# A six-stage transformer program: plain turned blocks and the causal projection's copy on ScalarE, the bias as a product of one row, and the first causal heads beside the last feed-forward

## The chip, the cores and the metric

The kernel runs on one core of one Trainium2 chip. The metric is the device time of one execution, in microseconds (us). A core has TensorE (PE in the profile; PEld is its weight load), VectorE (DVE), ScalarE (ACT), GpSimd (POOL) and SyncE (SP, whose queue issues the DMAs). PE writes its results to PSUM, which DVE and ACT read and POOL does not.

## What is computed

Eight sequences of 512 tokens with 256 features, float32, run through four residual layers. Cut to what matters:

```
x = x + latent_attention(layernorm(x))            # stage a, 8 heads
x = x + ffn_block(layernorm(x))                   # two layers f: local attention, feed-forward
x = x + causal_attention(layernorm(x))            # stage b, 16 heads of 16
x = x + ffn_block(layernorm(x))                   # two layers f

causal_attention(x):
    q, k, v = split(x @ w_qkv + b_qkv)
    dot = q @ k.T
    scores = dot * dot / (|q|^2 + |k|^2 - 2 dot + 1e-6)
    out = softmax(scores where key <= query) @ v
    return out @ w_out + b_out
```

## The kernel before

**Stages and units.** `PLAN` lists six stages: a, f, f, b, f, f. A stage runs over the 8 sequences; a stage of one sequence is a unit `u`, so that the causal stage b is units 24 to 31, and unit 23 is the last feed-forward unit before it. Attention is cut into steps: in stage b there are 24 steps `k` a unit. A step takes two heads; three steps (k%3 = 0, 1, 2) cover the query tiles 1 and 0, then 2, then 3 of these heads, with 384, 384 and 512 key columns a head.

**A causal step.** PE computes `bden` (denominators, 18 rows deep) and `bdot` (16 rows deep) into a pair of PSUM banks each (three pairs, `wide0` to `wide2`). DVE bounds the denominators (`bclip`), ACT squares the dots into a `prob` buffer (`bnum`) and makes a first guess of the reciprocal by Ln and Exp (`bguess`). DVE improves the guess (`bclose`, and the first half of `bmul`) and multiplies with a running maximum (second half of `bmul`). ACT takes the exponential (`exp`), PE turns the 128x128 blocks (`turn_a`, `turn_b`, transposes into one PSUM pair), ACT copies the first half to the buffer `pt` (`pt_a`, line 1209), DVE the second (`pt_b`): blocks on the diagonal times a 0/1 mask (line 1408), and for k%3 = 2 two blocks below the diagonal as a plain copy (line 1411). PE then forms the output (`mix`). `bclip`, `bguess`, `bclose` and `bmul` share three buffers `b_den` and `b_inv`, which lie in rooms (`w_up`, `x_2`, `hid`) that the feed-forward uses too.

**The projection of stage b.** For each of 4 token tiles PE forms 128x768 of q, k and v (`bqkv`: two halves of the depth, 512 and 256 columns each). DVE adds the bias, which a DMA has spread over all 128 rows of `w_in`, and writes the tile to `raw` (`row`, line 1324). ACT squares q and k (`bsq`, line 1144) and copies v to its place (line 1147), DVE sums the squares (`bss`, line 1331), and POOL puts q, k and the sums in rows (`brow`). After the four tiles PE turns the rows (`bk`, `bq`), ACT copies them (`bk_c`, `bq_c`), and SP copies the halves crosswise by DMA (`dup_a`, `dup_b`).

**The ends of a unit.** `sel`, `olog`, `osum`, four `fan` (PE, a product of 16 rows into the one bank `turn_ps`) and `out_b` (DVE, line 1425) normalise the output of a unit; `proj` and `res` (DVE, line 1431) add it to x. In a feed-forward unit follow `moved` (DMA), `bn_f`, `bn_f2`, `nrm_f`, `xt2`, three `up_g` with `gate`, `gelu` (ACT), three `up_h` with `hid`, four `down`, `res2` (DVE, line 1494), and `back` (POOL, line 1593).

**The order.** Nothing is issued by hand. `parts_of` lists the parts of each unit with a due time and what each follows; `cost` gives a length to each; `ordered` builds for each engine one fixed order. It always takes, among the parts that can start within `PATIENCE` (0.3) of the earliest, the one with the lowest due time, and gives PSUM rooms to PE's parts as their readers free them. The engines run these orders in program order, each waiting on semaphores. In stage b `bclip`, `bguess`, `bden` and the DMAs of the first steps follow unit 23's last `up_h`, `down` and `back`, since their buffers lie in that unit's rooms:

```
put("bden", k, at, ..., last, *turned, ("down", u - 1, 3))
put("bclip", k, at, final("bdot", k), ("bmul", *three), ("up_h", u - 1, 2))
put("bguess", k, at + .5 / steps, final("bclip", k), ("bmul", *three), ("down", u - 1, 3), ("back", u - 1, 0))
```

## Time and profile before

| | us |
|---|---|
| median of 3 runs (4489.77 to 4497.48) | 4490.21 |
| the profiled execution's own time | 4488.74 |
| its span, from first to last instruction | 4486.5 |
| stage b, from the first causal product to the next stage alone (about 1991 to 3150 in the span) | 1158.6 |

The time of an execution is its span and 2.24 us around it here. The page's first part gives each engine's busy time, the second cuts the span in 40 slices with the clock granted to TensorE, and the fifth lists groups of instructions by line. A line of a helper (823 for every product, 826 for every transpose, 1603 for every DMA) stands for many operations, so these are told apart by the names of their tiles and by their shapes. A product in float32 stands as two MATMUL records, a transpose as one.

### The profile page before, as it was taken

How to read it: one execution, taken by the hardware profiler on the slowest of the kernel's cores; microseconds unless marked ns; L12 is line 12 of the kernel's file. 1: busy time of each engine (PE TensorE's matmuls, PEld its weight loads, DVE VectorE, ACT ScalarE, POOL GpSimd, SP SyncE). 2: the span in 40 equal slices, each digit the busy share in tenths (PEclk: the TensorE clock that was granted, in tenths of full speed). 3: DMA queues.
4: the chain of work that ended last, by engine and by line, in shares of the span. 5: the costliest groups of instructions: out<-in, count | busy, mean ns of one | idle time of the engine just before them, and what ended most of it. 6: DMA issues, size and time to landing. Idle time of an engine off the chain costs nothing.

```text
span 4486.5 us, 65884 instructions
## 1 busy us (share of the span) xinstructions
PE 4149.7 (92%) x23120; PEld 2608.4 (58%) x23120; DVE 3315.1 (74%) x7977; ACT 2541.7 (57%) x5478; POOL 1658.1 (37%) x1816
## 2 busy tenths in 40 slices
PE   8999989999999999988888887888999999999997
PEld 5666556566566566555555555554566665665664
DVE  5667777777667667559999999998677776677662
ACT  4555554454454454439888888876454454454441
POOL 1222365445446456330000010013464464465541
PEclk9999999999999999987888889888999999999998
DMA  2000000000010000000000000101000000100000
GB/s 75 10 16 6 24 10 6 3 3 6 23 29 12 11 8 11 23 21 20 20 22 20 20 23 22 34 20 34 3 6 3 3 25 8 34 15 17 15 17 21
DMA packets 63095, 78.33 MB, mean 17 GB/s; under 512 B 15344, under 2 KB 47520, under 8 KB 62768
## 3 DMA queue, kind: packets, MB, share of 16 engines
q1 hardware_dynamic: 62768, 74.12, 5.8%
q8 instruction: 186, 3.05, 0.3%
q14 instruction: 141, 1.16, 0.1%
HBM read 36.37 MB, written 12.58 MB: 11 GB/s over the span
## 4 chain that ended last, share of the span: by engine, by line
PE 63%; DVE 23%; issue 6%; ACT 4%; POOL 2%; DMA 0%; SPq 0%; POOLq 0%; DVEq 0%; ACTq 0%
PE wide L823 43%; PE o_ps L823 7%; PE wide L826 6%; PE turn_ps L826 4%; DVE x L1246 3%; DVE turned L1297 2%; DVE w_up L1359 2%; PE turn_ps L823 2%; DVE prob L1371 2%; DVE x L1365 2%; DVE prob L1382 2%; DVE w_up L1344 1%; POOL prob L1575 1%; DVE turned L1283 1%; DVE hid L1365 1%
## 5 line engine op out<-in xcount | busy, mean ns | idle before, releaser
L823 PE MATMUL wide<-x,w_up 128*128 128x512 f32 (+5 forms) x2560 | 856.6, 552 | 5.5 <-DVE x L1463 4.1
L823 PE MATMUL wide<-w_in,x_t 128*128 128x512 f32 (+2 forms) x1920 | 811.7, 566 | 15.8 <-ACT q_t L1122 8.3
L1575 POOL TENSOR_SCALAR prob<-prob,st 128x256 f32<-128x256 f32 (+1 forms) x1024 | 496.3, 503 | 821.7 <-DVE st L1395 819.1
L1182 ACT ACTIVATE prob<-prob,st 128x256 f32<-128x256 f32 (+1 forms) x1024 | 479.2, 471 | 251.5 <-DVE st L1382 251.2
L823 PEld LDWEIGHTS wide<-w_in,x_t 128*128 128x128 f32 x1920 | 341.4, 192 | 368.6 <-issue 359.0
L823 PEld LDWEIGHTS wide<-x,w_up 128*128 128x128 f32 (+2 forms) x2560 | 377.2, 198 | 291.9 <-issue 279.3
L823 PE MATMUL o_ps<-pt,v 128*32 128x128 f32 (+2 forms) x5120 | 509.3, 345 | 16.8 <-DVE pt L1411 5.4
L1548 POOL TENSOR_TENSOR sines<-raw,rot 128x512 f32<-128x512 f32 x256 | 351.4, 1393 | 336.7 <-ACT raw L1110 336.4
L1556 POOL TENSOR_TENSOR rn<-ss,minus_half 128x16 f32<-128x16 f32 x128 | 423.1, 3305 | 103.3 <-DVE ss L1292 96.3
L823 PEld LDWEIGHTS o_ps<-pt,v 128*64 128x64 f32 (+1 forms) x5120 | 326.8, 133 | 227.1 <-issue 143.4
L1213 ACT ACTIVATE o_t<-o_ps 128x512 f32<-128x512 f32 x192 | 114.4, 596 | 521.2 <-PE o_ps L823 521.0
L1382 DVE CUSTOM_DVE_ANT_0 prob<-wide,local_mask 128x256 f32<-128x256 f32 (+1 forms) x1024 | 331.6, 384 | 61.3 <-PE wide L823 58.5
L823 PE MATMUL wide<-k_t,q_t 64*128 64x256 f32 (+2 forms) x2456 | 367.7, 413 | 1.7 <-DVE pt L1415 0.8
L823 PE MATMUL wide<-w_out,o_t 128*128 128x256 f32 x1536 | 351.7, 388 | 4.0 <-ACT o_t L1213 1.9
L826 PE MATMUL turn_ps<-ident,prob 128*128 128x128 f32 x1916 | 311.2, 280 | 31.1 <-ACT pt L1209 15.9
L826 PE MATMUL wide<-ident,prob 128*128 128x128 f32 x1844 | 294.1, 305 | 48.8 <-issue 15.6
L823 PE MATMUL wide<-hid 18*128 18x256 f32 (+3 forms) x1024 | 227.0, 531 | 120.5 <-DVE pt L1408 28.5
L823 PE MATMUL wide<-w_down,hid 128*128 128x256 f32 (+1 forms) x1536 | 332.7, 388 | 4.8 <-DVE hid L1486 4.8
L823 PEld LDWEIGHTS wide<-w_out,o_t 128*128 128x128 f32 x1536 | 298.8, 196 | 62.1 <-issue 14.8
L826 PEld LDWEIGHTS turn_ps<-ident,prob 128*128 128x128 f32 x1916 | 223.8, 141 | 183.7 <-issue 152.8
L1486 DVE SCALAR_TENSOR_TENSOR hid<-wide,bias_up,hid 128x512 f32<-128x512 f32 (+1 forms) x224 | 144.8, 669 | 250.7 <-ACT hid L1232 138.7
L826 PEld LDWEIGHTS wide<-ident,prob 128*128 128x128 f32 x1844 | 228.6, 155 | 164.5 <-issue 120.3
(153 smaller groups left out, 7490.1 us busy)
## 6 DMA issues: line engine op xcount, KB each, us to landing
kept<-resid SPq DMA_DIRECT2D x16, 512.0 KB, 3.0
x<-kept SPq DMA_DIRECT2D x16, 512.0 KB, 3.3
w_up<-hid SPq DMA_DIRECT2D x64, 128.0 KB, 2.2
x<-hid SPq DMA_DIRECT2D x64, 128.0 KB, 2.4
shifted<-resid SPq DMA_DIRECT2D x32, 224.0 KB
w_in<-in_f_wqkv SPq DMA_DIRECT2D x4, 1536.0 KB, 6.3
w_up<-in_f_w SPq DMA_DIRECT2D x4, 1492.0 KB, 6.7
resid<-in_x SPq DMA_DIRECT2D x8, 512.0 KB, 8.9
```

Of the source, the lines that this page charges most:

```text
L823: return eng.matmul(out, lhsT, rhs, start=start, stop=stop, skip_group_check=True)
L826: return eng.transpose(out, in_, ident[:, :])
L1182: last = eng.activation(pr[:, local_span(t)], pr[:, local_span(t)], ACT.Exp, bias=sm[:, t:t + 1], scale=-1.0, accum_out=sm[:, 4 + t:5 + t])
L1213: eng.activation(o_t[:, i, :], o_ps[:, :], ACT.Copy).then_inc(S["out"], 1)
L1246: return eng.tensor_scalar(dst, src, stat[:, 64 + 2 * t:65 + 2 * t], stat[:, 96 + t:97 + t], ALU.subtract, ALU.mult)
L1297: eng.tensor_tensor(out[:, :], out[:, :], sines[(o - 1) % 2][:, :], ALU.add).then_inc(S["add"], 1)
L1365: eng.scalar_tensor_tensor(out=inv, in0=den, scalar=2.0, in1=inv, op0=ALU.subtract, op1=ALU.mult).then_inc(S["binv"], 1)
L1382: eng.tensor_tensor_reduce(pr[:, local_span(t)], ps[:, local_span(t)], local_mask[:, P if t == 0 else 0:256], -1.0, LOW, ALU.add, ALU.min, ...
L1486: last = eng.scalar_tensor_tensor(out=hid[rows, m, cols], in0=ps[rows, 512 * k + cols.start:512 * k + cols.stop], scalar=bias_up[rows, m:m ...
L1548: last = eng.tensor_tensor(halves(sines[(o - 1) % 2][:, side]), halves(r[:, side])[:, :, ::-1, :], rot[:, 2 * z + 1, i, :].rearrange("p (u ...
L1556: eng.tensor_tensor(rn[(o - 1) % 2][:, 0:16], ss[(o - 1) % 2][:, 0, :], minus_half[:, 0:16], ALU.pow).then_inc(S["rn"], 1)
L1575: last = eng.tensor_scalar(pr[:, local_span(t)], pr[:, local_span(t)], sm[:, 8 + t:9 + t], 1.0, ALU.mult, ALU.mult)
```

## The change

Four edits, and the planner's tables with them.

1. **Plain blocks by ScalarE.** For k%3 = 2 the two blocks below the diagonal are copied by ACT in a new part `pt_c`, which waits for `pt_b` (DVE, the masked blocks of the same bank) and for which `mix` and the reuse of the PSUM pair wait.
2. **The bias by a product.** The bias stays one row; a row of ones (`one_row`, a new input) is loaded beside it, and PE adds the bias by a product of depth 1 with 512 and 256 columns at the end of each `bqkv`.
3. **The copy by ScalarE.** `row` moves from DVE to ACT, and copies q and k alone (512 columns). `bsq` reads PSUM in place of `raw`, and no longer waits for `row`; the PSUM pair is held until both are done.
4. **The first causal heads.** The steps k = 0, 1, 2 of unit 24 take other buffers (`prob2`, `prob3`, `sines`), and no longer wait for unit 23's `down`, `up_h` and `back`. They run one at a time there (each waits for the `bmul` of the step before). The parts of unit 23's feed-forward get the due time 23.9 each.

The core of the diff:

```diff
+def early(u, k):
+    return u == FIRST_B and k < 3
+def early_group(u, k):
+    return u == FIRST_B and k < 6
...
+        if early(u, k):
+            n_prob = 2
...
-        "ACT": "fold_q_c xt_c raw v_c q_c aq_c av_c bsq bk_c bq_c bnum bguess exp pt_a out olog gelu",
-        "DVE": "fold_o_c bn_h nrm_h cos ss join k_c ak_c row bss bclip ...
+        "ACT": "fold_q_c xt_c raw v_c q_c aq_c av_c bsq row bk_c bq_c bnum bguess exp pt_a pt_c out olog gelu",
+        "DVE": "fold_o_c bn_h nrm_h cos ss join k_c ak_c bss bclip ...
...
-            put("bsq", i, at, final("row", i), ("bss", *back1), ...
+            put("bsq", i, at, final("bqkv", i), ("bss", *back1), ...
...
-            put("bden", k, at, final("bk_c", g), final("bq_c", g), final(dup, g), last, *turned, ("down", u - 1, 3))
+            ffn = [] if early(u, k) else [("down", u - 1, 3), ("up_h", u - 1, 2), ("back", u - 1, 0)]
+            put("bden", k, at, final("bk_c", g), final("bq_c", g), final(dup, g), last, *turned, *ffn[:1])
...
-            put("bclip", k, at, final("bdot", k), ("bmul", *three), ("up_h", u - 1, 2))
+            if early(u, k):
+                three = (u, k - 1)
+                ffn = [("turn_a", u - 1, STEPS["f"] - 1), ("turn_b", u - 1, STEPS["f"] - 1)]
+            put("bclip", k, at, final("bdot", k), ("bmul", *three), *ffn)
...
+            if k % 3 == 2:
+                put("pt_c", k, at + 2 / steps, final("pt_b", k), *mixed)
-            put("mix", k, at + 3 / steps, final("pt_a", k), final("pt_b", k), final("bsq", 3), o_free)
+            put("mix", k, at + 3 / steps, final("pt_a", k), final("pt_b", k), final("pt_c", k), final("bsq", 3), o_free)
...
+    after = lambda late: u + .9 if u == FIRST_B - 1 else u + 1 + late
...
-                            last = mm(ps[:, lo:lo + w], x_t[:, c, 1 + i * P:1 + (i + 1) * P], w_in[:, at:at + w],
-                                      c == 0, c == FC - 1)
+                            mm(ps[:, lo:lo + w], x_t[:, c, 1 + i * P:1 + (i + 1) * P], w_in[:, at:at + w], c == 0, False)
+                    for lo, w in ((0, 512), (512, 256)):
+                        last = mm(ps[:, lo:lo + w], one_row, qkv_bias[:, lo:lo + w], False, True)
...
+                elif kind == "row":
+                    act.wait_ge(S["bqkv"], o)
+                    act.wait_ge(S["brow"], o - 2)
...
+                    eng.activation(raw[(o - 1) % 2][:, 0:2 * DIM], wide[PLACE["bqkv", u, i]][:, 0:2 * DIM], ACT.Copy
+                                   ).then_inc(S["row"], 1)
                 elif kind == "bsq":
-                    act.wait_ge(S["row"], o)
+                    act.wait_ge(S["bqkv"], o)
...
+                elif kind == "pt_c":
+                    act.wait_ge(S["pt_b"], nth("pt_b", u, i))
+                    met, n = P * B_OWN[i % 3], P * len(B_TURNS[i % 3][1])
+                    eng.activation(prob_t[SLOTS[u, i]["pt"]][:, 512 + met:512 + n],
+                                   wide[PLACE["turn_b", u, i]][:, 512 + met:512 + n], ACT.Copy).then_inc(S["pt_c"], 1)
...
-                elif kind == "row":
-                    row = raw[(o - 1) % 2]
...
-                    eng.tensor_tensor(row[:, 0:3 * DIM], wide[PLACE["bqkv", u, i]][:, 0:3 * DIM], qkv_bias, ALU.add
-                                      ).then_inc(S["row"], 1)
...
-                        if n > met:
-                            last = eng.tensor_copy(pt[:, 512 + met:512 + n], ps[:, 512 + met:512 + n])
```

The fixed orders differ only from unit 22 to unit 34. Two places show how.

**PE, between the attention of unit 23 and its `down`.** `wide<-x_2,w_up` are the feed-forward's `up_g` and `up_h`, `wide<-w_in,x_t` the causal projection, `w_down,hid` is `down`. Before, behind the last `up_g` tile:

```order
L823 MATMUL wide1<-x_2,w_up 106x256 x4
L823 MATMUL wide1<-x_2,w_up 128x512 x2
L823 MATMUL wide2<-w_in,x_t 128x512
L823 MATMUL wide2<-w_in,x_t 128x256
L823 MATMUL wide2<-w_in,x_t 128x512
L823 MATMUL wide2<-w_in,x_t 128x256
L823 MATMUL wide0<-x_2,w_up 128x512 x4
L823 MATMUL wide2<-x_2,w_up 128x512 x4
L826 MATMUL wide1<-ident,turned0 128x128 x8
L823 MATMUL wide0<-w_down,hid 128x256 x24
```

and with the change (`sines` hold the first causal rows, `w_in` alone is the product of one row):

```order
L876 MATMUL wide0<-w_in,x_t 128x512
L876 MATMUL wide0<-w_in,x_t 128x256
L876 MATMUL wide0<-w_in,x_t 128x512
L876 MATMUL wide0<-w_in,x_t 128x256
L876 MATMUL wide0<-w_in 128x512
L876 MATMUL wide0<-w_in 128x256
L876 MATMUL wide2<-x_2,w_up 128x512 x4
L876 MATMUL wide1<-x_2,w_up 128x512 x4
L876 MATMUL wide0<-sines0 128x512 x2
L876 MATMUL wide2<-sines1 128x512 x2
L876 MATMUL o_ps<-pt0,v0 32x128 x6
L876 MATMUL wide1<-w_down,hid 128x256 x24
```

The products of step 2 and the `mix` of step 0 (and in front of this piece the products of steps 0 and 1 and the transposes of step 0) now stand ahead of `down`; the transposes of unit 26's layernorm (`ident,turned0`) and, further on, two of its four projections, which stood there or right behind, come later.

**ACT, around a `bsq` and a step with k%3 = 2 in the middle of unit 27.** Before:

```order
L1163 ACTIVATE prob0<-wide1 128x768
L1144 ACTIVATE turned1<-raw0 128x512
L1147 ACTIVATE v0<-raw0 128x16x16
L1209 ACTIVATE pt1<-wide0 128x256
L1174 ACTIVATE x_2<-w_up 128x768
L1176 ACTIVATE x_2<-x_2 128x768
L1163 ACTIVATE prob1<-wide1 128x768
```

and with the change:

```order
L1199 ACTIVATE raw0<-wide1 128x512
L1206 ACTIVATE turned1<-wide1 128x512
L1209 ACTIVATE v0<-wide1 128x16x16
L1270 ACTIVATE pt1<-wide0 128x256
L1260 ACTIVATE st3<-st3 128x2
```

and a dozen rows further on

```order
L1270 ACTIVATE pt1<-wide0 128x512
L1235 ACTIVATE hid<-w_up 128x1024
L1237 ACTIVATE hid<-hid 128x1024
L1274 ACTIVATE pt1<-wide0 128x256
L1227 ACTIVATE prob3<-wide2 128x768
```

`row` (L1199) stands in one piece with `bsq`, all three reading the same PSUM pair, and `pt_c` (L1274) stands two activations behind its step's `pt_a`. The ACT order also holds two more table loads (61 before, 63 now): unit 23's `gelu` now stands between causal steps, with a load ahead of it and one behind.

## Rows read from the trace of the kernel before

**Rows 1.** Page: busy shares, and granted clock in 40 slices

```profile
PE 4149.7 (92%) x23120; PEld 2608.4 (58%) x23120; DVE 3315.1 (74%) x7977; ACT 2541.7 (57%) x5478; POOL 1658.1 (37%) x1816
...
PEclk9999999999999999987888889888999999999998
```

**Rows 2.** Windows; us, then PE, PEld, DVE, ACT, POOL busy, clock, DMA, GB/s

```profile
2000.00:2100.00 100.00, 80.07 (x653) 51.80 (x646) 98.98 (x233) 95.97 (x171) 0.00 (x0) 0.76 0.09 21
...
1991.40:3150.00 1158.60, 954.31 (x7022) 602.23 (x7024) 1071.48 (x2448) 969.14 (x1725) 126.98 (x160) 0.85 0.09 23
```

**Rows 3.** Windows of one causal sequence (137.5 us), and of its parts

```profile
2411.00:2548.50 137.50, 112.32 (x857) 71.10 (x856) 128.94 (x296) 117.74 (x208) 11.19 (x18) 0.87 0.08 20
...
2421.00:2509.00 88.00, 66.29 (x588) 43.62 (x588) 86.38 (x208) 83.05 (x148) 5.33 (x13) 0.92 0.10 25
...
2509.00:2538.40 29.40, 25.93 (x172) 14.09 (x170) 27.45 (x59) 25.25 (x44) 5.87 (x5) 0.85 0.08 19
...
2538.40:2558.00 19.60, 19.60 (x100) 13.04 (x98) 15.21 (x33) 9.44 (x17) 0.00 (x0) 0.70 0.00 1
```

**Rows 4.** Waits over two sequences, 2411 to 2687 us: total, times, longest

```profile
DVE o_t L1425 <- PE turn_ps L823: 7.1, 5, 2.6
...
ACT st L1199 <- DVE st L1371: 16.5, 19, 2.2
```

**Rows 5.** Groups of the stretch 2421 to 2509 us: count, busy, mean ns, idle before

```profile
L1365 DVE SCALAR_TENSOR_TENSOR x<-w_up,x 128x768 f32<-128x768 f32 x12 | 11.4, 951 | 0.2
...
L1365 DVE SCALAR_TENSOR_TENSOR hid<-w_up,hid 128x1024 f32<-128x1024 f32 x5 | 6.1, 1211 | 0.0
...
L1324 DVE TENSOR_TENSOR raw<-wide,w_in 128x768 f32<-128x768 f32 x3 | 2.9, 950 | 0.0
...
L1411 DVE COPY pt<-wide 128x256 f32<-128x256 f32 x6 | 2.5, 412 | 0.0
```

**Rows 6.** Groups by form, 1950 to 2850 us

```profile
L1209 ACT ACTIVATE pt<-wide 128x256 f32<-128x256 f32 x51 | 19.2, 377 | 10.1 <-PE wide L826 9.9
...
L1209 ACT ACTIVATE pt<-wide 128x512 f32<-128x512 f32 x100 | 58.7, 587 | 2.4 <-PE wide L826 2.3
...
L823 PE MATMUL wide<-hid 18*128 18x256 f32 x208 | 48.7, 489 | 50.3 <-DVE pt L1411 17.1 <-ACT prob L1163 11.3 <-issue 9.6
```

**Rows 7.** Timelines of DVE and ACT: start, us, what, idle before it

```profile
2506.81 0.41 DVE L1411 COPY pt<-wide 128x256 f32<-128x256 f32 x1
...
2507.14 1.22 DVE L1359 TENSOR_TENSOR w_up<-w_up,hid 128x1024 f32<-128x1024 f32 x1
...
2518.62 0.96 DVE L1324 TENSOR_TENSOR raw<-wide,w_in 128x768 f32<-128x768 f32 x1 [1.61 <-PE wide L823]
...
2003.51 0.38 ACT L1209 ACTIVATE pt<-wide 128x256 f32<-128x256 f32 x1
...
2003.78 0.20 ACT L1199 ACTIVATE st<-st 128x2 f32<-128x2 f32 x1
```

**Rows 8.** Timeline of PE: a projection's tile, and one fan product

```profile
1987.48 2.75 PE L823 MATMUL wide<-w_in,x_t 128*128 128x512 f32 x8
...
2545.08 1.91 PE L823 MATMUL turn_ps<-shifted,w_down 16*128 16x512 f32 x2
```

**Rows 9.** The change of stage: window, and PE, DVE, POOL, SP timelines

```profile
1922.90:1991.40 68.50, 63.38 (x229) 39.51 (x230) 38.00 (x87) 14.55 (x27) 28.98 (x43) 0.98 0.11 25
...
1973.71 10.34 PE L823 MATMUL wide<-w_down,hid 128*128 128x256 f32 x48 [0.72 <-DVE hid L1486]
...
2003.07 0.42 DVE L1344 TENSOR_SCALAR w_up<-wide 128x256 f32<-128x256 f32 x1
...
2007.67 0.69 DVE L1371 CUSTOM_DVE_ANT_0 prob<-prob,hid 128x512 f32<-128x512 f32 x1
...
1985.46 2.35 POOL L1593 TENSOR_TENSOR resid<-resid,x 128x1024 f32<-128x1024 f32 x1 [7.05 <-DVE resid L1494]
...
1988.34 0.56 SPq L1603 DMA_DIRECT2D w_up<-hid  x1
```

More of the change, by code:

```diff
@@ L152, in cost @@
         n = len(B_TURNS[i % 3][kind[-1] == "b"])
-        return {"turn": 0.03 + 0.152 * n, "pt_a": 0.06 + 0.117 * n, "pt_b": (0.2 if i % 3 == 2 else 0.1) + 0.118 * n}[
+        return {"turn": 0.03 + 0.152 * n, "pt_a": 0.06 + 0.117 * n, "pt_b": 0.1 + 0.118 * (2 if i % 3 == 2 else n)}[
             "turn" if kind[0] == "t" else kind]
+    if kind == "pt_c":
+        return 0.3
     if kind in B_COST and st == "b":
@@ L304, in parts_of @@
                     free = (u, 6 * (g - 1) - 1) if g >= 2 else (u - 1, 6 * (g + 3) - 1)
-                    put(kind + "_c", g, at - 4 / steps, final(kind, g), ("bdot", *free), ("down", u - 1, 3))
+                    put(kind + "_c", g, at - 4 / steps, final(kind, g), ("bdot", *free),
+                        ("join" if early_group(u, k) else "down", u - 1, 3))
                 for half in range(2):
@@ L374, in parts_of @@
         return out
-    put("bn_f", 0, u + 1, final("res"), ("nrm_f", max(v for v in range(-1, u) if v < 0 or stage_of(v) == "f"), 0))
-    put("moved", 0, u + 1, final("res"), ("nrm_f", u - 1, 0))
-    put("bn_f2", 0, u + 1, final("bn_f"), final("moved"), ("pad_down", n * SEQS, 0))
-    put("rstd_f", 0, u + 1, final("bn_f2"))
-    put("nrm_f", 0, u + 1, final("rstd_f"), ("bmul", u - 1, BSTEPS - 1), ("xt2", u - 1, 0), ("back", u - 1, 0))
-    put("bias", 0, u + 1.2, final("nrm_f"), ("load_up", n * SEQS, 0))
@@ L382, in parts_of @@
-    put("xt2", 0, u + 1.2, final("nrm_f"))
-    put("xt2_c", 0, u + 1.2, final("xt2"), ("up_h", u - 1, 2), ("load_up", n * SEQS, 0))
+    after = lambda late: u + .9 if u == FIRST_B - 1 else u + 1 + late
+    put("bn_f", 0, after(0), final("res"), ("nrm_f", max(v for v in range(-1, u) if v < 0 or stage_of(v) == "f"), 0))
+    put("moved", 0, after(0), final("res"), ("nrm_f", u - 1, 0))
+    put("bn_f2", 0, after(0), final("bn_f"), final("moved"), ("pad_down", n * SEQS, 0))
+    put("rstd_f", 0, after(0), final("bn_f2"))
@@ L439, in readers_of @@
     if kind == "turn_a" and stage_of(u) == "b":
-        last.append(("pt_b", u, i))
+        last += [("pt_b", u, i), ("pt_c", u, i)]
     if kind == "score" and stage_of(u) == "f":
@@ L573 @@
         "load_fold fold_q fold_q_c fold_o fold_o_c aq aq_c lat ak_c av_c bqkv row bsq bv bss brow bk bk_c bq bq_c bias_b "
-        "score bden bdot low inv exp wt wt_b bclip bnum bln bguess bclose binv bmul turn_a turn_b neg pt_a pt_b mix sel fan out olog oexp osum out_b load_sel "
+        "score bden bdot low inv exp wt wt_b bclip bnum bln bguess bclose binv bmul turn_a turn_b neg pt_a pt_b pt_c mix sel fan out olog oexp osum out_b load_sel "
         "proj res moved bn_f bn_f2 var_f rstd_f nrm_f bias xt2 xt2_c up_g gate gelu up_h hid down res2 back_in back store "
@@ L637, in build, with rows_home, close_home, close_free @@
         k_rows = [b_hid[:, 1024 + 512 * i:1536 + 512 * i] for i in range(2)]
+        early_rows = [sines[0][:, 0:512], sines[0][:, 512:1024], sines[1][:, 0:512], sines[1][:, 512:1024]]
+        def rows_home(u, g):
+            return early_rows if early_group(u, 6 * g) else [q_rows[g % 2], k_rows[g % 2], q_half, k_half]
+        def close_home(u, i):
+            pair = [prob["prob2"], prob["prob3"]] if early(u, i) else [a[(nth("bguess", u, i) - 1) % 3] for a in (b_den, b_inv)]
+            return [a[:, 0:2 * b_width(i)] for a in pair]
+        def close_free(gate, u, i):
+            if early(u, i):
+                gate.wait_ge(S["bmul"], nth("bmul", u, i) - 1)
+                gate.wait_ge(S["turn_a"], nth("turn_a", u - 1, STEPS["f"] - 1))
+                gate.wait_ge(S["turn_b"], nth("turn_b", u - 1, STEPS["f"] - 1))
+            else:
+                gate.wait_ge(S["bmul"], nth("bmul", u, i) - 3)
+                if u == FIRST_B:
+                    gate.wait_ge(S["down"], nth("down", u - 1, TILES - 1))
+                    gate.wait_ge(S["up_h"], nth("up_h", u - 1, len(UP_H) - 1))
+                    gate.wait_ge(S["back"], nth("back", u - 1))
         b_weight = shifted[0:BHEADS, :, :].rearrange("p t n -> p (t n)")
@@ L1162, in scalar_program @@
                     prob_free(act, u, i)
+                    if u == FIRST_B and not early(u, i):
+                        act.wait_ge(S["bmul"], nth("bmul", u, 2))
                     eng.activation(two(prob[SLOTS[u, i]["prob"]][:, 0:2 * w], slice(0, w)),
```

110 lines of the change are left out of this document (56 added, 54 removed).

## The prediction

> **What bounds the kernel now.** I read the page first. PE is busy for 92% of the span, DVE for 74%, ACT for 57% [rows 1], so PE seems to be the bound. It is not everywhere. The slices of granted clock fall below 9 from the 18th on for about a quarter of the span [rows 1], and the windows show why: in the causal stage b DVE is busy for 99 us of a window of 100 us, ACT for 96, PE for 80 [rows 2]. Over the whole stage of 1158.6 us DVE is busy 1071.5 (92%), ACT 969.1 (84%), PE 954.3 (82%) [rows 2]. The change works in this stage and at its start, so its worth is read there.
>
> One causal sequence takes 137.5 us, with 128.9 of DVE, 117.7 of ACT and 112.3 of PE [rows 3]. It has two kinds of stretch. In a long one of 88 us nothing but steps runs: DVE 86.4 (98%), ACT 83.1 (94%), PE 66.3. Around the sequence's end the next 29.4 us have DVE at 27.5, ACT at 25.3 and PE at 25.9, and in the last 19.6 us PE never rests while DVE is busy for 15.2 and ACT for 9.4, at a mean granted clock of 0.70 [rows 3]. DVE's waits are in this last part: 7.1 us in two sequences for the fan products [rows 4]. ACT's waits are for DVE: 16.5 us in two sequences for the maxima of `bmul` [rows 4]. So DVE is the bound of the long stretch, with ACT close behind it, and PE of the last one.
>
> **Term 1, DVE.** The plain copy goes: 412 ns each [rows 5], but the next instruction starts 0.33 us after it [rows 7], and that is what it occupies. 8 a sequence, 64 in all: 21.1 us. `row` goes: 950 ns each [rows 5], 0.87 us with the same overlap of 0.08, 4 a sequence, 32 in all: 27.8 us. DVE also waited 1.61 us for PE ahead of one of them [rows 7], a wait that goes to ACT. Together 6.1 us of 128.9 a sequence.
>
> **Term 2, ACT.** `pt_c` is the copy of 256 columns that ACT makes already for k%3 = 0: 377 ns [rows 6], 0.27 us to the next start [rows 7]; 64 of them, 17.3 us. `row` now copies 512 columns: 587 ns for that form [rows 6], less the same overlap of 0.11 us, 0.48 us; 32 of them, 15.4 us. `bsq` and the copy of v read PSUM in place of SBUF; I count no gain or loss for them. That is 4.1 us more a sequence: 121.8, against 122.8 for DVE. The two engines become equal.
>
> What the row shows here is that for this copy out of PSUM ACT is not slower than DVE (377 against 412 ns). The Trainium skill (ScalarE: Activation LUTs, Rules for kernel authors) says that additions and the like should go to VectorE, which per element is up to about three times faster in bf16; by that the 64 copies would cost ACT some 79 us in place of 17, and ACT would be far above DVE. The trace disagrees for float32 from PSUM, and the sum keeps its rows.
>
> **Term 3, PE.** A projection tile streams 2 x 768 columns in 2.75 us at full clock [rows 8]. The products of one row stream 768 more: 1.37 us, 32 times, 44 us on PE. No row has a product of depth 1. The nearest, the fan product of 16 rows, takes 1.91 us for 512 columns where the clock stands at the lower level [rows 8], so few rows save nothing, and 768 columns would take 2.8 us there. Bounds: 1.37 and 2.8 us; I take 1.37, since most tiles lie where the clock is mostly full. In the long stretch PE is idle for 21.7 of 88 us [rows 3], which hides it. If that cover were gone, it would be 4 times 1.4 to 2.8 us a sequence.
>
> **Term 4, the held pair.** `pt_c` waits for `pt_b`, and `mix` and the PSUM pair for both. Before, the pair was free 0.33 us after the masked product; now after a hop to ACT, whatever ACT is doing, and 0.38 us. PE's products of the next step waited on the old copy for 17.1 us in 900 [rows 6]. So this wait exists already, 0.3 us a time. I count nothing, because PE has 25% to spare in these stretches; its bounds are 0 and one ACT instruction (1 us) a time, 8 us a sequence.
>
> **Term 5, the change of stage.** From the end of unit 23's attention to the first causal product PE is busy 63.4 of 68.5 us, DVE only 38.0, ACT 14.6 [rows 9]. `down` ends at 1984.05 [rows 9]. Now eight products of one row (11.0 us) and about half the PE work of three steps (a step has about 4 us of PE in the long stretch, 66.3 us for its 17 steps [rows 3, 5]; so 6 us) stand ahead of that end, and unit 26's transposes (1 us) behind it: it comes 16 us later, at about 2000. `res2` and `back` (1.4 us to the start of `back`, and 2.35, [rows 9]) then hold step 3 until about 2004, against 2003.07 before; but steps 0 to 2 are through DVE by then, which before was at 2008.4 [rows 9]. What is gained by DVE is the work between (about 4 us), less 1. The two extra table loads are on ACT, which is idle there. On SP four DMAs of the first heads are now ahead of `moved`, 0.56 us each to issue [rows 9], up to 2.3 us; PE has unit 25's projections to do meanwhile. I take 0 for the whole, with bounds of 5 us either way: the early heads pay for the products of one row, no more.
>
> **The sum.** Long stretch (17 steps, 12 and 5 of them by the widths of line 1365, with 6 plain copies and 3 `row`, [rows 5]): DVE falls by 6 x 0.33 + 3 x 0.87 = 4.6 to 81.8, ACT rises by 6 x 0.27 + 3 x 0.48 = 3.1 to 86.1. ACT is now the higher. Filled to 98% as DVE is today, it needs 87.9 us, a gain of 0.1; if it were no bound, DVE at 98% would need 83.5, a gain of 4.5. I take 99%, which DVE reaches in a window where ACT has 96% [rows 2]: 87.0 us, a gain of 1.0. End of the sequence: DVE loses one `row` with its wait (0.87 + 1.61) and two copies (0.66), 3.1 us; PE is nearly full there, so 1.4 of that goes to the product of one row. A gain of 1.7. Together 2.7 us a sequence, 8 sequences: 22 us. Against the profiled execution's 4488.7 that is 4466.7; the median of the runs stands 1.5 us above it, so **4468**.
>
> **The rivals.**
> - **A, the forecast: ACT and DVE share the bound.** 15 to 30 us faster, 4460 to 4475. For it: the balance of the two sums. Chance 0.40.
> - **B, DVE's relief comes through whole.** ACT's waits for DVE (8 us a sequence, [rows 4]) show it has room that opens as DVE gets faster, and 4 to 6 us a sequence come out: 32 to 48 us, 4442 to 4458. Against it: ACT at 94 to 96% already. Chance 0.27.
> - **C, ACT takes DVE's place.** ACT in order, at 122 us with 12 us of unavoidable waits, gives 134 to 137.5 with the later PSUM pairs eating the rest: within 9 us, 4481 to 4494. The early heads may also do nothing, since they only trade places with unit 26's projections. Chance 0.18.
> - **D, PE becomes the bound: slower.** The place is the sequence's end, where PE never rests. At the lower clock a product of one row costs 2.8 us; and in the trace the clock falls to that level after the fan products, which are 16 rows deep. If the products of depth 1 bring more time at the lower level, as after the fans, PE does its work there at twice the time. It decides when PE's work plus this passes DVE's relief of 6.1 us a sequence: four tiles with 1.4 more each make 5.6, and half of the 5.9 us of clock that the last stretch loses now (0.30 of 19.6 us, [rows 3]) makes it 8.5. The loss is 2.4 to 3 us a sequence, some 22 in all, 4512. Against it: PE's 25 us of idle a sequence. Chance 0.15. The Trainium skill (TensorE: Matmul & The Clock Gate, Part 4) says that a transpose does not count as busy for the clock in the way a product does. Stage b, full of transposes, has a mean clock of 0.85 [rows 2], which agrees, and no row tells whether a depth of 1 counts.
>
> That the change does not do what it says I leave out: the orders show each part moved.
>
> **How the numbers follow.** 0.2% of the time, 9 us, is about what a measurement of this kernel tells from no change. Faster by more: nearly all of A and B, 0.66, and a little of C, 0.68. Within: most of C and the edge of A, 0.18. Slower: D less what it may turn to nothing, 0.14. The range of 8 in 10 runs from the middle of B, 4442, to the upper edge of C, 4493; the forecast's own is 4458 to 4476.
>
> **What would show it.** In the page after: DVE's busy time lower by about 55, ACT's higher by about 43 us, PE's by 44 or more. In the windows of a sequence in mid-stage: about 134.8 us, DVE 122 to 123, ACT 122. In the groups: a one-row product of 512 columns as long as other products of 512; `pt_c` near 380 ns. In the waits: DVE's wait ahead of `row` gone, and PE's `<-DVE pt L1411` now on ACT, no longer in total. At the change of stage: `down` ending near 2000, step 3 at about 2004. The prediction is wrong if sequences stay at 137 us with ACT above 95% throughout (C), if they fall below 132 (B), or if the mean clock of stage b falls under 0.82 (D).

## The result, and the profile after

The changed kernel takes **4543.31 us** (median of 4 runs, 4539.49 to 4547.61) against 4489.99 for the kernel before on the same chip: ratio **1.0117**, 95% interval 1.0104 to 1.013, a loss of 53 us. The forecast was 4468, the range 4442 to 4493: wrong in sign, and outside the range. Even the slower rival, D, stood at 4512.

The page of the kernel after (span 4543.0 us; the profiled execution took 4544.86), with its busy shares, its granted clock in 40 slices and the shares of the chain that ended last:

```profile
PE 4224.6 (93%) x23248; PEld 2639.0 (58%) x23248; DVE 3278.2 (72%) x7881; ACT 2576.7 (57%) x5576; POOL 1659.2 (37%) x1816
...
PEclk9999999999999999997888888888999999999999
...
PE 66%; DVE 16%; ACT 9%; issue 6%; POOL 2%; DMA 0%; SPq 0%; POOLq 0%; DVEq 0%; ACTq 0%
```

Against [rows 1] DVE has 37 us less, ACT 35 more and PE 75 more, where 55, 43 and 44 were foretold. To place the loss I cut the stage by the 1.22 us addition of `res` that ends each sequence's attention. Its starts in units 24 and 30 are 2149.18 and 2970.38 us before, 2161.61 and 3033.16 after. So the stage stands 12 us later at the end of its first sequence and **loses 50 us in the six sequences that follow** (821 against 872). Of the 12, 5.5 were there before anything differed: the fixed orders differ only from unit 22 on, and the `back` of unit 21 started at

```profile
1839.47 2.36 POOL L1593 TENSOR_TENSOR resid<-resid,x 128x1024 f32<-128x1024 f32 x1 [0.65 <-DVE resid L1494]
```

before and, after, at

```profile
1844.96 2.36 POOL L1645 TENSOR_TENSOR resid<-resid,x 128x1024 f32<-128x1024 f32 x1 [0.64 <-DVE resid L1546]
```

At this point the twenty profiled executions of all kernels here lie between 1838.2 and 1845.0, so starts in two traces are compared by their distance from it. At unit 31's `res` the changed kernel is 65 us behind (3126.06 and 3191.39); the rest of the span gives 9 of them back, which leaves the 56.5 of the two profiled spans. The windows of the six sequences (us, then PE, PEld, DVE, ACT, POOL busy, clock, DMA, GB/s), before:

```profile
2149.00:2970.00 821.00, 676.11 (x5157) 430.56 (x5158) 774.28 (x1772) 706.75 (x1248) 67.42 (x106) 0.87 0.09 23
```

and after, with one sequence in the middle (from `res` of unit 27 to that of unit 28) behind it:

```profile
2161.00:3033.00 872.00, 738.67 (x5285) 457.89 (x5283) 751.15 (x1709) 731.66 (x1325) 63.26 (x108) 0.85 0.08 22
...
2595.00:2744.00 149.00, 125.05 (x895) 77.61 (x894) 128.17 (x289) 123.95 (x224) 14.01 (x22) 0.84 0.09 23
```

The sequence of 137.5 us with DVE at 94% [rows 3] has become this one of 149 us with DVE at 86%, ACT at 83% and PE at 84%: nobody is full, and it is slower. It is one of the longer ones; from `res` to `res` the six take 145.3 us on average, 136.9 before. DVE did get its relief (774 to 751). PE is busy for 62.6 us more, while its idle time went from 145 to 133 us. So the loss of 51 is PE's busy time less 12 of idle; that is a sum and not yet a cause. The one-row products of these 24 tiles make 41 of the 63 (26.9 and 14.2 in the rows below), and the rest goes with a clock of 0.85 in place of 0.87. The groups of the kernel after by form, 1950 to 2850 us, show the new operations (count, busy, mean ns, idle before them):

```profile
L876 PE MATMUL wide<-w_in 1*128 1x512 f32 x48 | 26.9, 640 | 0.0
L1274 ACT ACTIVATE pt<-wide 128x256 f32<-128x256 f32 x47 | 17.3, 367 | 2.8 <-DVE pt L1462 2.8
...
L876 PE MATMUL wide<-w_in 1*128 1x256 f32 x48 | 14.2, 374 | 0.0
L1199 ACT ACTIVATE raw<-wide 128x512 f32<-128x512 f32 x24 | 14.1, 589 | 25.0 <-PE wide L876 25.0
```

Their sizes are as foretold: `pt_c` 367 ns (377 [rows 6]), the row copy 589. The largest of PE's waits from 1990 to 3100 us (total, times, longest), after:

```profile
PE o_ps L876 <- ACT pt L1274: 33.4, 20, 2.7
PE wide L879 <- ACT pt L1274: 27.1, 15, 2.9
PE wide L876 <- ACT pt L1274: 19.6, 9, 3.0
PE wide L876 <- DVE w_up L1400: 14.1, 16, 1.8
```

and before, in the same stretch:

```profile
PE wide L823 <- DVE pt L1408: 28.7, 20, 2.6
PE wide L823 <- DVE w_up L1346: 18.8, 23, 1.8
PE wide L823 <- DVE pt L1411: 18.4, 6, 3.5
```

80 us of PE's waits now end with `pt_c` (L1274), and 12 more with DVE's mask (L1462); before, 61 ended with DVE's two turned copies (47 in the rows above, the rest in four smaller ones). The timeline shows how one arises (start, us, engine, what, idle before it):

```profile
2339.36 0.59 ACT L1270 ACTIVATE pt<-wide 128x512 f32<-128x512 f32 x1
...
2339.84 1.06 ACT L1235 ACTIVATE hid<-w_up 128x1024 f32<-128x1024 f32 x1
2340.02 0.42 DVE L1462 TENSOR_TENSOR pt<-wide,causal_keep 128x256 f32<-128x256 f32 x1
...
2340.93 1.06 ACT L1237 ACTIVATE hid<-hid 128x1024 f32<-128x1024 f32 x1
...
2341.89 0.37 ACT L1274 ACTIVATE pt<-wide 128x256 f32<-128x256 f32 x1
...
2342.40 1.97 PE L876 MATMUL wide<-w_in,x_t 128*128 128x512 f32 x2 [1.36 <-ACT pt L1274]
```

DVE's mask is done at 2340.44, but ACT has the Ln and Exp of the next `bguess` (2 x 1.06 us) ahead of `pt_c` in its fixed order, and the PSUM pair comes free 1.8 us after the mask. In the plan 61 of the 64 `pt_c` stand directly behind a `bguess`. My first theory was this handover, with the one-row products and the early heads as rivals.

### The profile page after: what moved, and what is told of

Read it like the earlier page. It is cut to its first block, busy times and chain, and to the rows that moved or that the text cites. A ratio compares the mean times of both kernels' runs of the same rounds, so it can differ in the third digit from the quotient of the medians.

```text
span 4543.0 us, 66166 instructions
## 1 busy us (share of the span) xinstructions
PE 4224.6 (93%) x23248; PEld 2639.0 (58%) x23248; DVE 3278.2 (72%) x7881; ACT 2576.7 (57%) x5576; POOL 1659.2 (37%) x1816
## 4 chain that ended last, share of the span: by engine, by line
PE 66%; DVE 16%; ACT 9%; issue 6%; POOL 2%; DMA 0%; SPq 0%; POOLq 0%; DVEq 0%; ACTq 0%
PE wide L876 45%; PE o_ps L876 8%; PE wide L879 7%; PE turn_ps L879 4%; DVE x L1312 2%; DVE turned L1363 2%; PE turn_ps L876 2%; ACT prob L1263 2%; DVE prob L1436 1%; POOL prob L1627 1%; ACT prob L1227 1%; ACT pt L1270 1%; DVE turned L1366 1%; ACT hid L1235 1%; DVE turned L1349 1%
## 5 line engine op out<-in xcount | busy, mean ns | idle before, releaser
L876 PE MATMUL wide<-w_in,x_t 128*128 128x512 f32 (+2 forms) x1920 | 834.5, 580 | 30.9 <-ACT pt L1274 14.2
L876 PE MATMUL wide<-x,w_up 128*128 128x512 f32 (+3 forms) x2528 | 856.3, 551 | 3.1 <-DVE x L1515 1.7
L876 PEld LDWEIGHTS wide<-w_in,x_t 128*128 128x128 f32 x1920 | 351.0, 197 | 396.5 <-issue 386.1
L876 PEld LDWEIGHTS wide<-w_down,hid 128*128 128x128 f32 (+1 forms) x1536 | 255.1, 189 | 55.6 <-issue 22.1
```

What stands on the lines that cost most here:

```text
L876: return eng.matmul(out, lhsT, rhs, start=start, stop=stop, skip_group_check=True)
```

## The experiments

Eighteen kernels ran. Differences in us are the ratio less 1, times 4490; the interval in brackets behind each ratio is a 95% interval, and one of plus or minus 0.0015 is 7 us. A difference between two of these kernels carries both intervals, about 9 us. The table at the end of this section has all of them.

### The edits apart (e1 to e4)

The edits of the diff were taken as three (the one-row products and ScalarE's row copy together are the bias edit), singly and in combination; the planner orders each anew. `e1_without_plain` is the changed kernel with the `pt_c` edit undone:

```
-                put("pt_c", k, at + 2 / steps, final("pt_b", k), *mixed)
...
+                        if n > met:
+                            last = eng.tensor_copy(pt[:, 512 + met:512 + n], ps[:, 512 + met:512 + n])
```

> The changed kernel with the plain blocks given back to VectorE (no pt_c; mask and plain copy both at pt_b); the one-row products, ScalarE's row copy and the early heads stay. Theory P (the handover VectorE to ScalarE holds the mix and the PSUM pair: in the changed kernel PE idles some 60 us of 1950 to 2850 behind L1274): most of the loss of 53 us goes, 4470 to 4500 us. Rival Q (the one-row products, 640 ns a record of 512 columns where I had counted less, make PE the bound and bring the clock down): the loss stays, 4530 to 4550. Rival R (the early heads disturb the order of the whole stage): also 4530 or more here, and the run with the early heads alone is slower as well.

`e2_plain_alone`, the kernel before with only the `pt_c` edit:

> The kernel before with one edit alone: the plain blocks of every third head by ScalarE as pt_c. Theory P: slower than before by 30 to 50 us (4520 to 4540), with PE idle behind the pt_c line and the sequences of the causal stage at 143 to 150 us. Rivals Q and R: VectorE loses 64 x 0.33 = 21 us and nothing is added to PE, so 4465 to 4490.

`e3_bias_alone`, only the one-row products and ScalarE's copy:

> The kernel before with one edit alone: the bias by products of one row, the copy of 512 columns by ScalarE. Theory P: VectorE is relieved by 28 us, PE gets 45 us that mostly lie in its idle time: 4470 to 4495. Rival Q: slower, 4510 to 4540, PE busy in the causal stage over 90% and its clock lower for longer.

`e4_early_alone`, only the early heads:

> The kernel before with one edit alone: the first three causal heads may run beside the last feed-forward. Theory P: 4480 to 4495, the step between the two stages moves by under 10 us. Rival R: 4505 or more, mostly at the change of stage, where the changed kernel's end of the last feed-forward came 20 us later.

Measured: e1 1.0019 (1.0006 to 1.0031), e2 1.0004 (0.9988 to 1.002), e3 1.0056 (1.0034 to 1.0077), e4 1.0005 (0.9991 to 1.002). The handover as sole cause falls: alone it costs nothing measurable. The bias edit alone costs 25 us. The plan of e2 has 62 of its 64 `pt_c` directly behind a `bguess`, as the changed kernel's has 61, so that place alone isn't what costs. Early heads alone do nothing, and e1, which has them, is only 9 us slower than before: R falls. But the parts don't add up: the plain copy costs nothing beside the old code or beside the early heads (`v4_plain_and_early`, 1.0005, 0.9995 to 1.0015), and 44 us beside the bias edit and the early heads (1.0117 against 1.0019). Of the combinations one did not run: plain copy and bias edit without the early heads.

> The kernel before with the plain blocks by ScalarE and the early heads, and without the bias edit. Each of the two alone moved the time by under 3 us. If the order made with the plain copy in it goes bad only beside the one-row products: 4485 to 4500. If it goes bad with the early heads: 4515 or more.

The early heads have a use after all: from the `back` of unit 21 to `res` of unit 24 e3 takes 319.5 us and e1 305.6, where the kernel before takes 309.7. So they give back 14 us at the change of stage, where the bias edit had cost 10. Both are small for one trace: orders of the old computation (o1 to o3 below) spread from 304.5 to 316.6 us at this place. In the whole time the early heads are worth 16 us there (1.0056 against 1.0019).

### One operation out, the order untouched (e5, e6, f3)

To tell operations from order, the next kernels keep the changed kernel's order, place for place. `e5_no_products` leaves out the products:

```
-                    for lo, w in ((0, 512), (512, 256)):
-                        last = mm(ps[:, lo:lo + w], one_row, qkv_bias[:, lo:lo + w], False, True)
...
```

> The changed kernel, its order untouched, without the one-row products: the bias of the causal projection is left out of the computation (its load stays), 64 records of PE less. The four runs before this one showed that the plain blocks alone and the early heads alone move nothing and that the bias edit alone costs 24 us, so the theories are put anew. Theory Q (PE's time: 2 x 0.5 us a tile, 32 tiles, and the clock that falls with them): 4500 to 4520 here, 25 to 45 us less than the changed kernel. Rival O (the cost lies in the order that the planner makes from the new set of parts, and in its waits between engines): 4535 to 4545, under 10 us less.

`e6_plain_back` keeps the products, lets DVE do the plain copy behind its mask, and leaves ACT's place empty:

```
                 elif kind == "pt_c":
...
+                    pass
...
+                        if n > met:
+                            last = eng.tensor_copy(pt[:, 512 + met:512 + n], ps[:, 512 + met:512 + n])
```

> The changed kernel, its order untouched, with the plain copy done by VectorE right behind the mask, and ScalarE's place for it left empty. Theory H (the handover from VectorE to a ScalarE whose queue holds the 2.1 us of the next Ln and Exp ahead of it costs some 1 us a head on PE's path, 64 heads): 4495 to 4515. Rival O (the order itself): 4535 to 4555, since VectorE gets its 21 us back and the order stays.

Measured: e5 1.0042 (1.0025 to 1.0058), 34 us below the changed kernel. e6 1.0092 (1.0076 to 1.0108), 11 us below it. So giving the handover back is worth 11 us here (by the two intervals, 2 to 20), and that is net of the 64 copies that DVE does again; leaving the products out is worth 34. But e6 holds the same instructions as e1 (PE x23248, DVE x7945, ACT x5512 in both pages), and e1 is 33 us faster: **the order and the PSUM places that the planner makes when `pt_c` is among its parts cost three times what the handover itself does.** The traces put 16 of them in the six sequences (842 and 858 us) and 12 between unit 21's `back` and unit 24's `res` (305.6 and 317.4 us). `f3_neither` takes both the handover and the products out of the changed kernel's order:

> The changed kernel's order with both parts of its cost taken out: the plain copy by VectorE, ScalarE's place for it empty, and no one-row products (the bias is left out of the computation). If the two parts add up (34 and 11 us apart): 4495 to 4502, and what is left above before is the order and ScalarE's place in the bias edit. If they cover each other: 4503 to 4510.

It took 1.0095 (1.0076 to 1.0113): not faster than e6, and 24 us slower than e5. Neither of the two foretold sums came. In this order the products cost 34 us where ScalarE copies the blocks and nothing where DVE does, and giving the copy back to DVE gains 11 with the products and loses 24 without them. No run leaves the copy out altogether in this order. Six sequences of e5, of e6 and of f3:

```profile
2146.00:3000.00 854.00, 697.28 (x5196) 440.29 (x5198) 752.02 (x1711) 729.44 (x1326) 67.06 (x108) 0.85 0.09 22
```

```profile
2162.00:3020.00 858.00, 730.36 (x5272) 454.55 (x5270) 765.92 (x1759) 719.16 (x1282) 69.10 (x108) 0.85 0.08 22
```

```profile
2152.00:3021.00 869.00, 713.50 (x5173) 449.37 (x5170) 765.63 (x1758) 720.44 (x1278) 71.47 (x108) 0.83 0.08 22
```

From e6 to f3 PE loses its products but only 17 us of busy time, because the clock falls from 0.85 to 0.83, and it idles 27 us more (155 against 128). The clock's fall isn't a chance of one execution: over the whole span the four executions of e6 have 0.949 to 0.953, the four of f3 0.945 or 0.946.

### One operation in or out, in the order of before (b1, v1, e8)

`b1_products_only` puts the one-row products into the kernel before, loads the bias as one row, and turns DVE's addition into a copy at the same place:

```
-                    eng.tensor_tensor(row[:, 0:3 * DIM], wide[PLACE["bqkv", u, i]][:, 0:3 * DIM], qkv_bias, ALU.add
-                                      ).then_inc(S["row"], 1)
+                    eng.tensor_copy(row[:, 0:3 * DIM], wide[PLACE["bqkv", u, i]][:, 0:3 * DIM]).then_inc(S["row"], 1)
...
```

> The kernel before, its order untouched, with the bias as one-row products and VectorE's addition over 768 columns turned into a copy over the same columns at the same place: PE's part of the edit alone. Theory Q (PE's time and clock): 4505 to 4520. Rival O: 4488 to 4500, the 32 x 1.0 us of PE lying in its idle time.

Measured 1.0047 (1.0027 to 1.0067), 21 us (12 to 30). The page says PE is busy for 4195.9 us, 46.2 more than before: 1.44 us a tile, of which 0.66 us shows in the time. The groups of b1, 1950 to 2850 us, have the products beside the deep ones of the same 24 tiles:

```profile
L823 PE MATMUL wide<-w_in,x_t 128*128 128x512 f32 x96 | 54.2, 648 | 0.0
L823 PE MATMUL wide<-w_in,x_t 128*128 128x256 f32 x96 | 29.0, 384 | 0.0
L823 PE MATMUL wide<-w_in 1*128 1x512 f32 x48 | 26.9, 640 | 0.0
L823 PE MATMUL wide<-w_in 1*128 1x256 f32 x48 | 14.2, 374 | 0.0
```

By these rows the products themselves are 41.1 us for 24 tiles, 1.71 us each.

`v1_no_plain_copy` takes DVE's plain copy away and puts nothing in its place: the relief of DVE with no price. It leaves those blocks uncopied.

```
-                        if n > met:
-                            last = eng.tensor_copy(pt[:, 512 + met:512 + n], ps[:, 512 + met:512 + n])
```

> The kernel before, its order untouched, with VectorE's copy of the plain blocks left out of the computation (64 copies of 412 ns; the mask multiplication stays, and nothing takes the copy's place). If VectorE's time bounds the causal stage: 4465 to 4470, 20 to 25 us less than before. Rival L (the stage is bound by a ring of waits among the engines in their fixed order, in which PE's time counts as well): 4478 to 4492, under half of it.

Measured 0.9984 (0.9975 to 0.9994): **7 us (3 to 11) for 64 copies of 412 ns**, 21 by my count. This is the run that decides over the forecast. Four sequences of before:

```profile
2282.00:2830.00 548.00, 448.72 (x3436) 285.43 (x3436) 516.26 (x1185) 470.66 (x832) 46.91 (x75) 0.87 0.08 21
```

and of v1:

```profile
2288.00:2831.00 543.00, 460.57 (x3425) 291.72 (x3424) 506.15 (x1152) 471.58 (x832) 46.58 (x75) 0.84 0.08 22
```

DVE lost 10.1 us, the stretch 4 (547.2 to 543.2 from `res` to `res`), and PE, with the same work, is 11.9 us busier at a clock of 0.84 in place of 0.87. This last is one execution against one, and too little to build on: over the whole span the ten executions of v1 have a clock of 0.953 to 0.956 and the 21 of before beside them 0.952 to 0.959, means of 0.954 and 0.955. Where the other 14 us of DVE's relief went these two traces don't say.

`e8_plain_old_order` puts `pt_c` right behind `pt_a`, in the order of before:

> The kernel before, its order untouched, with the plain copy by ScalarE right behind its copy of the other half of that head, where it waits for VectorE's mask with ScalarE's queue behind it. If VectorE bounds the stage and the handover costs little when no Ln and Exp stand before it: 4470 to 4482. If the bound is the ring of waits among three engines and not VectorE's time: 4488 to 4500. If the handover costs a microsecond a head wherever it stands: above 4510.

Measured 1.0244 (1.0228 to 1.026), 110 us. The wait is where the handover was put, and ACT's queue stands behind it. ACT's waits from 2150 to 3050 us:

```profile
ACT pt L1220 <- DVE pt L1420: 81.8, 46, 6.9
ACT prob L1170 <- PE wide L829: 54.6, 24, 6.1
```

So the place behind Ln and Exp, which I had blamed, was far better than this one.

### The rest of the bias edit (v3)

`v3_act_copy_no_bias` is e3 without its products, in the same fixed order:

> The bias edit alone (4516 us) without its one-row products: the bias is left out of the computation, ScalarE copies the 512 columns, VectorE has no addition. Theory Q (the loss of the edit is PE's time): 4488 to 4496, as before or a little less. If ScalarE's place in the edit costs by itself: 4505 or more. If VectorE's relief of 28 us counts in full: 4465.

Measured 1.0031 (1.0019 to 1.0042), 14 us slower than before, between the foretold values. Of the 25 us of e3 the products are 11 (about 0 to 22, by the two intervals); and 14 remain with DVE relieved by 28 and PE having no more to do. Its six sequences:

```profile
2154.00:2991.00 837.00, 707.00 (x5157) 445.35 (x5156) 758.63 (x1744) 711.61 (x1273) 71.56 (x108) 0.83 0.09 23
```

PE does the work of before (x5157 in both) in 31 us more, at 0.83 where it was 0.87. Here the other executions agree: over the whole span the six of v3 have a clock of 0.947 to 0.952, the 21 of before beside them 0.952 to 0.959. Idle time fell by 15 us at once (145 to 130), and the window grew by 16. The order is another than before's, so how much of this is ScalarE's place and how much the order stays open.

### Is it the luck of one order? (o1 to o4)

Three kernels keep the computation of before and give the planner the changed kernel's numbers, so that in 326 to 454 places of PE's, ACT's and DVE's orders another part stands. The first (o1) changes one number, the second (o2) gives the projection's parts the changed kernel's (`bqkv` 4.2 for 3.3, `bsq` 0.8 for 0.82, `row` 0.52 for 0.85), the third (o3) both, and a fourth kernel (o4) plans the changed computation with other numbers. The edit of o1:

```
-"pt_b": (0.2 if i % 3 == 2 else 0.1) + 0.118 * n
+"pt_b": 0.1 + 0.118 * (2 if i % 3 == 2 else n)
```

> The kernel before with nothing of its computation changed: only the planner's number for the turned copy is the changed kernel's (pt_b of every third head 0.34 instead of 0.67), so the order of the causal stage is another. If the planned order by itself is worth tens of microseconds: off by more than 10 us from before, on either side. If orders of the same instructions are all about as good, and what costs is the handover and PE's time: within 7 us of before.

> As the last, with the changed kernel's numbers for the bias edit (bqkv 4.2, bsq 0.8, row 0.52) and the computation of before. The bias edit without its products cost 15 us though it relieved VectorE by 28. If those 15 are the order that these numbers make: 4500 to 4515. If they are ScalarE's place in the edit: 4483 to 4495.

> Both sets of numbers at once, the computation of before. Order theory: another value again, more than 10 us from before or from the two runs ahead. Otherwise within 7 us of before.

> The changed kernel's computation in full, planned with other numbers (bqkv 3.3 instead of 4.2, pt_c 0.4 instead of 0.3). If the 31 us between the two orders of one computation (plain copy at VectorE: 4532 in the changed kernel's order, 4500 in its own) are the luck of one order: 4505 to 4530. If they belong to any order that hands the plain copy over beside the one-row products: 4535 to 4550.

Measured: o1 0.9992 (0.9979 to 1.0006), o2 0.9997 (0.9986 to 1.0008), o3 1.0006 (0.9995 to 1.0016); o4 1.0095 (1.008 to 1.0111). Orders of the old computation differ by a few us in the whole time; their six sequences spread more (821, 817 and 833 us, against 821 before). The changed computation, ordered with other numbers, gains 10 on the changed kernel and still loses 43. So it is hardly the luck of one order: all three orders made for parts with both edits (after, o4 and h10 below) lose 43 us or more, and the one order of e1, without `pt_c`, 9.

### The place of the handover (h10, g10)

One number of the plan moves the turned copies forward, `pt_c` with them:

```
-                put("pt_" + side, k, at + 2 / steps, final("turn_" + side, k), *mixed)
+                put("pt_" + side, k, at + 1.0 / steps, final("turn_" + side, k), *mixed)
...
```

> The changed kernel with one number of the plan changed: pt_a, pt_b and pt_c fall due one step's share earlier, so the mask comes earlier at VectorE, and pt_c stands behind the Ln and Exp of bguess in 22 places of 64, not in 61. If that place is what makes the handover and the order dear: 4500 to 4525. If any order with the handover beside the products costs as much: 4530 to 4550.

> The same earlier due times with the plain copy by ScalarE and the early heads, without the bias edit (behind bguess in 19 places of 64 instead of 61; 4491 us with the old due times). If the place of the handover is what ate the relief of VectorE: 4470 to 4485, the best so far. If VectorE's relief is worth nothing anyhow: 4486 to 4500.

Measured: h10 1.0167 (1.015 to 1.0185), 22 us slower than the changed kernel; g10 1.0022 (1.001 to 1.0035), 8 us slower than v4. Getting most of the handovers out from behind Ln and Exp made both worse. Both runs move every turned copy and so the whole order, so they don't price the place by itself; but with e2 and v4, which have 62 and 61 of 64 in that place and lose nothing, and with e6, they leave nothing for that theory.

### All runs

Windows are six sequences, from `res` of unit 24 to that of unit 30; PE idle is the window less PE's busy time. "Order" tells whose plan it is. Each window is of the one profiled execution (that of e2 took 4502.7 us, 11 more than the median of its ten), and orders of one computation spread from 817 to 833 here, so the ratio decides and not the window.

| run | what it is | order | ratio | us from before | window | PE busy | PE idle | DVE busy | clock |
|---|---|---|---|---|---|---|---|---|---|
| before | | own | 1 | 0 | 821 | 676 | 145 | 774 | 0.87 |
| v1 | no plain copy | before | 0.9984 | -7 | 818 | 686 | 132 | 760 | 0.86 |
| b1 | products | before | 1.0047 | +21 | 829 | 702 | 127 | 777 | 0.88 |
| e8 | `pt_c` at `pt_a` | before | 1.0244 | +110 | 913 | 733 | 180 | 760 | 0.80 |
| e2 | `pt_c` | own | 1.0004 | +2 | 826 | 696 | 130 | 757 | 0.84 |
| e4 | early heads | own | 1.0005 | +2 | 820 | 676 | 144 | 774 | 0.87 |
| v4 | `pt_c`, early | own | 1.0005 | +2 | 824 | 691 | 133 | 756 | 0.85 |
| g10 | v4, earlier due | own | 1.0022 | +10 | 837 | 685 | 152 | 761 | 0.84 |
| v3 | ACT's row copy | own | 1.0031 | +14 | 837 | 707 | 130 | 759 | 0.83 |
| e3 | that and products | own | 1.0056 | +25 | 841 | 725 | 116 | 756 | 0.86 |
| e1 | e3 and early | own | 1.0019 | +9 | 842 | 720 | 122 | 761 | 0.87 |
| e6 | as e1 | after | 1.0092 | +41 | 858 | 730 | 128 | 766 | 0.85 |
| f3 | e6, no products | after | 1.0095 | +43 | 869 | 714 | 155 | 766 | 0.83 |
| e5 | all, no products | after | 1.0042 | +19 | 854 | 697 | 157 | 752 | 0.85 |
| after | all | own | 1.0117 | +53 | 872 | 739 | 133 | 751 | 0.85 |
| o4 | all, other numbers | own | 1.0095 | +43 | 864 | 717 | 147 | 752 | 0.87 |
| h10 | all, earlier due | own | 1.0167 | +75 | 886 | 767 | 119 | 748 | 0.80 |

(o1, o2 and o3: -4, -1, +3.) Read the columns together: every kernel with `pt_c`, with ACT's row copy or with the copy left out has DVE 8 to 26 us less busy, and none but v1 has a shorter window, by 3 us. No version beat both kernels by more than a measurement can tell, unless it left work out.

## Why the prediction was wrong

**"So DVE is the bound of the long stretch" failed first, and with it the step from busy time to time.** The sum let a stretch be as long as the busy time of its fullest engine, filled to 99% as in one window of 100 us [rows 2], and at the sequence's end it took DVE's relief less one product as time. From 49 us of relief at DVE against 33 more on ACT it so got its 22. The changed kernel's six sequences are filled to 86% by DVE and to 84% by ACT (751 and 732 of 872 us): the busy times came about as forecast (ACT 121.9 us a sequence for 122, DVE 125.2 for 122 to 123), the fill did not. v1 measures the step by itself, with no load moved anywhere: 21 us off DVE, 7 gained. v3, with 28 of the relief and no products, was 14 slower. My reading is that the engines, in fixed orders through one another's results, are members of a ring, of which DVE at 98% was the fullest, with ACT at 94% beside it; no run shows the ring as such. And PE's time isn't fixed: in v3 and in f3 it did the same or less work at a lower granted clock.

**Term 1 and term 2: near.** DVE fell by 37 on the page, where the sum had 49 and the sign to look for 55: v1 lowers it by 18 and v3 by 25, near the 21 and 28 of the sum, and the changed kernel has less than these two together. ACT rose by 35 (33 in the sum, 43 as the sign), and `pt_c` took 367 ns. The page of the Trainium skill (ScalarE: Activation LUTs, Rules for kernel authors) would keep additions and the like off ScalarE, with its factor of three for bf16; carried over to these float32 copies, which its rule doesn't name, it gave my estimate of 79 us, and the run shows 64 x 0.37 = 24, with 367 ns on ScalarE where DVE took 412. So the factor doesn't hold for this copy. It would have led to the right sign by a wrong mechanism.

**Term 3: the duration was a quarter short, "hides it" was wrong.** 1.37 us a tile was taken, the price at the full clock; the products' own rows give 1.71, within the bounds of 1.37 and 2.8. PE's idle time was to hide it. It hid all of it from e6 to f3, and let 11 us through in e3 against v3, 21 in b1, and 34 in the changed kernel against e5. That a product stands in front of the operand that a waiting engine needs next is my reading of this; no row isolates it.

**Term 4, "I count nothing", failed.** Its upper bound, one ACT instruction a time, was too low as well: in the timeline above it is two. Yet in the changed order the handover costs 11 us net (e6), 0.17 us a copy, which lies within the bounds of the term as a whole (0 to 64); most of the 80 us of waits took the place of others, for PE's idle time fell. What had no term at all is that the planner, given `pt_c` as a part and the pair held for it, makes another order for the whole stage: 33 us (e6 against e1).

**Term 5: 0 within 5 us.** Right for the early heads by themselves (e4), and right that they pay for the products (e3 to e1, 14 us at that place). In the whole change `down` ends at 2004.55 and step 3 starts at 2009.26; less the 5.5 us by which this execution was late before, that is 1999 and 2003.8, where 2000 and 2004 were forecast and 2003.07 was step 3's start before [rows 9]. The steps after that are slower already: `res` of unit 24 comes 7 us late, net.

**The rivals.** D had the right sign and PE as its engine, at the wrong place and price: a tile's products do not cost 2.8 us, and the clock of the six sequences fell only from 0.87 to 0.85, not under 0.82. C, that ACT takes DVE's place, is refuted by ACT's share: 84%, below the 95 it asked for, with sequences of 145 us and not 137. B fell with v1. No rival had several small losses that add up, and none said that the order would be worse; I wrote that the orders "show each part moved" and priced only the parts.

**The account of the 53 us.** Walking by kernels: the bias edit 25 (11 of it products, 14 ACT's place and the order), the early heads beside it -16, the order made with `pt_c` +33, the handover +11. Each step is measured within some 9 us, but the steps depend on the way walked: the products are worth 34 us with the handover in the changed kernel's order and nothing without it (e6, f3). What stays open is which feature of that order costs the 33: other due times of the turned copies (h10) and other numbers for the planner (o4) did not take it away, and no run held one order and changed only the PSUM places.

## What to carry to other kernels

- The fullest engine, at 94% beside two at 86 and 82, was not a bound that pays out what is taken from it. Before costing a relief, run the kernel with that work simply left out: here it gave a third, which would have been a warning.
- A wait added between two engines of a planned kernel has three prices: the hop, the queue that stands before or behind it, and the order that the planner then makes. The last was the largest here. The same operations in two orders tell it (e6 against e1).
- Work put on an engine with idle time is not free when the idle time is many short waits. The same products cost 0, 11, 21 and 34 us in four settings here, of some 44 to 55 us of their own (32 tiles at 1.37 to 1.71).

## What the runs showed of the hardware

- A product of depth 1 costs what a deep one of the same width does. In b1, in the same tiles, it took 640 ns a record of 512 columns and 374 of 256, and the products 128 rows deep 648 and 384, all at a mixture of both clock levels. No row of before had one.
- A copy of 128x256 float32 out of PSUM took 367 ns on ScalarE and 412 on VectorE.
- PE's mean granted clock followed the schedule, and I had counted it as constant. With DVE relieved and PE's work unchanged (v3, in another order) it was 0.947 to 0.952 over the whole span, 0.952 to 0.959 before, and PE was busy for 31 us more in six sequences. Leaving the products out lowered it in one pair of kernels of equal order (0.949 to 0.953 in e6, 0.945 or 0.946 in f3) and raised it in another (0.948 to 0.950 in the changed kernel, 0.951 to 0.953 in e5). What tips it I can't tell from these runs: f3 idles more than e6 in the six sequences (155 against 128 us) at a lower clock, and v3 less than before (130 against 145), also at a lower one, so it is not simply idle time.
